# An eight-layer attention and feed-forward stack on one core: moved waits, a shared expert first on batch 0, batch 1 normalised later

## The reference, cut to what matters

```
x = x + L0_xattn(layernorm(x), ctx)   # top-32 attention gives FiLM factors, a state-space convolution by DFT, a GELU FFN
x = x + L0_ffn(layernorm(x))          # router picks 4 of 16 heads per batch item, then 512 x 512 self-attention
x = x + L1_xattn(layernorm(x), ctx)   # one head; scores normalised by mean and variance over the whole batch item
x = x + L1_ffn(layernorm(x))          # ternary signatures pick one of 64 table rows per token (argmax of a spline gate, twice)
x = x + L2_xattn(ctx, layernorm(x))   # two heads, x attends to x and to the context
x = x + L2_ffn(layernorm(x))          # 8 experts, top 2 weighted by softmax, plus 2 shared experts, hidden 256
x = x + L3_xattn(layernorm(x), ctx)   # 16 heads, 77 keys
x = x + L3_ffn(layernorm(x))          # ternary weights, hidden 512, GELU, layernorm inside
```

## Time and profile before

| what | value |
|---|---|
| median of three timed runs | 590.55 us (587.39, 590.55, 593.42) |
| the profiled execution's own time | 593.67 us |
| its span, first to last instruction | 591.9 us |
| mean granted TensorE clock | 0.896 of full speed |
| busy: TensorE matmul, VectorE, ScalarE, GpSimd | 86%, 65%, 46%, 26% |

### The profile page before, as it was taken

One profiled execution on the slowest core, in us unless ns is written; L12 is line 12 of the kernel. 1 busy time (PEld: TensorE's weight loads), 2 busy tenths in 40 slices (PEclk: granted clock), 3 DMA queues, 4 the chain that ended last, 5 costly groups with the idle time before them and its releaser, 6 DMA issues.

```text
span 591.9 us, 9329 instructions
## 1 busy us (share of the span) xinstructions
PE 510.3 (86%) x3141; PEld 351.9 (59%) x3141; DVE 383.6 (65%) x1362; ACT 272.2 (46%) x842; POOL 152.2 (26%) x179
## 2 busy tenths in 40 slices
PE   4931899999888999988879779989999999789976
PEld 2310899896434667765455457755666666358845
DVE  4899979466763668437666547753444444689766
ACT  2887675404135666432424426622222221678553
POOL 5999970301380000003004600100000000200042
PEclk9665599999989999998858959969999999789989
DMA  7002000003540000000001120000000000000001
GB/s 275 30 18 125 2 2 2 1 1 142 234 176 0 3 1 2 2 1 0 20 14 43 41 56 1 2 1 2 1 1 0 1 0 2 1 1 0 3 0 37
DMA packets 8198, 18.37 MB, mean 31 GB/s; under 512 B 1044, under 2 KB 6228, under 8 KB 7639
## 3 DMA queue, kind: packets, MB, share of 16 engines
q1 hardware_dynamic: 8150, 17.78, 8.4%
HBM read 15.99 MB, written 1.79 MB: 30 GB/s over the span
## 4 chain that ended last, share of the span: by engine, by line
PE 63%; DVE 14%; POOL 12%; ACT 5%; issue 3%; DMA 1%; SPq 0%; DVEq 0%; POOLq 0%; ACTq 0%
PE bank L1779 6%; PE bank L1780 6%; PE bank L1790 6%; PE bank L248 3%; PE bank L1026 3%; PE bank L1965 3%; PE bank L765 3%; PE bank L1070 3%; PE bank L1049 2%; PE bank L1941 2%; ACT arenaB L1981 2%; POOL rstd L206 2%; DVE stats L197 2%; PE bank L1653 2%; PE bank L679 2%
## 5 line engine op out<-in xcount | busy, mean ns | idle before, releaser
L205 POOL TENSOR_SCALAR rtmp<-mv 128x4 f32<-128x4 f32 x22 | 5.1, 230 | 326.3 <-DVE mv L191 326.3
L1831 DVE TENSOR_TENSOR arenaB<-arenaB,bank 128x512 f32<-128x512 f32 x40 | 27.5, 688 | 55.0 <-PE bank L1780 54.1
L1801 ACT ACTIVATE arenaB<-bank 128x512 f32<-128x512 f32 x40 | 23.9, 598 | 77.0 <-PE bank L1779 77.0
L1790 PEld LDWEIGHTS bank<-arenaA,arenaB 128*128 128x128 f32 x320 | 38.7, 192 | 9.1 <-issue 9.1
L248 PE MATMUL bank<-in_ctx 128*128 128x512 f32 (+1 forms) x114 | 43.4, 528 | 0.0
L1779 PE MATMUL bank<-xnT,arenaA 128*128 128x512 f32 x80 | 42.8, 618 | 0.0
L1780 PE MATMUL bank<-xnT,arenaA 128*128 128x512 f32 x80 | 42.0, 607 | 0.0
L1790 PE MATMUL bank<-arenaA,arenaB 128*128 128x128 f32 x320 | 38.8, 275 | 0.0
L248 PEld LDWEIGHTS bank<-in_ctx 128*128 128x128 f32 x114 | 20.2, 210 | 17.7 <-issue 17.6
L1981 ACT ACTIVATE arenaB<-bank,arenaB 128x77 f32<-128x77 f32 x88 | 27.2, 345 | 7.6 <-DVE arenaB L2004 7.6
L1780 PEld LDWEIGHTS bank<-xnT,arenaA 128*128 128x128 f32 x80 | 15.8, 197 | 20.2 <-issue 20.2
(11 more groups left out here) (472 smaller groups left out, 1260.8 us busy)
## 6 DMA issues: line engine op xcount, KB each, us to landing
arenaA<-in_moe_dram SPq DMA_DIRECT2D x1, 3840.0 KB, 11.7
in_dft<-in_dft_dram SPq DMA_DIRECT2D x1, 2048.0 KB, 7.4
in_dft<-in_head_dram SPq DMA_DIRECT2D x1, 2048.0 KB, 7.5
arenaA<-in_l_dram SPq DMA_DIRECT2D x1, 2048.0 KB, 16.2
vw_scratch<-in_dft SPq DMA_DIRECT2D x32, 38.5 KB
arenaB<-vw_scratch SPq DMA_DIRECT2D x2, 576.0 KB, 4.9
in_rows<-in_rows_dram SPq DMA_DIRECT2D x1, 842.5 KB, 7.3
in_ctx<-in_ctx_dram SPq DMA_DIRECT2D x1, 653.0 KB, 4.9
```

Of the source, the lines that this page charges most:

```text
L1790: ins = nc.tensor.matmul(bank[4 + m % 3][:, q4 * P:(q4 + 1) * P], hid2[:, m % 2, c, q4 * P:(q4 + 1) * P], w[:, 2 * HE + c * P:2 * HE + (c ...
L1801: nc.scalar.activation(sil2[:, n % 3, :], bank[n % 2][:], ACT.Silu).then_inc(silu_ready, 1)
L1831: Vv.tensor_tensor(hid2[:, m % 2, c, :], sil2[:, n % 3, :], bank[2 + n % 2][:], ALU.mult).then_inc(hid_ready, 1)
```

## The change

1. **Route.** The context keys are scaled, transposed and copied inside the route (`vec_c2_scale` after L930, `pe_c2_keys` after L915, `act_c2_keys` after the Exp). The spins are 2 and 5 calls instead of 3 and 8. The values of batch 1 are computed at step n = 1 of `attend0`, whose first wait is then for queries and keys alone. GpSimd waits for `heads_ready` before `pool_bias(3)` and the ternary weights.
2. **Moments.** A new `vec_tile_moments` does one tile's statistics. In `attend0`, `attend2` and `attend3` batch 1's moments are taken tile by tile inside the loop.
3. **L1_xattn.** Batch 0's copy and output product come before the last tiles; additions and moments go by batch item; the spin after it is 3 calls, not 4.
4. **L1_ffn.** The addition for `comp` and the second Exp each stand ahead of what was before them (`first_best`, `fold3` chunk 0); one spin of 2 calls is gone; both transposes precede all table products.
5. **L2_xattn into L2_ffn.** Batch 0 is normalised and turned inside `attend2` (steps 8 and 9). The experts start with shared expert 8 on batch 0; batch 1 is turned at step 2, the router products stand at step 4, and the choice of the best two is spread over steps 4 to 7 of VectorE's loop; its Exp becomes a power on GpSimd.
6. **L3.** `vec_normalise(9, [1])` moves from ahead of `attend3` into its step 1, after tile 0's product; `vec_normalise(10, [1])` into step 1 of `l3f`. Batch 0's turn for `l3f` goes into `attend3`'s last step.
7. **Stores.** Three groups of four: batch 0, batch 1's first two tiles, its last two.

```diff
+        def vec_tile_moments(st, src, t):
+            st.link(nc.vector.bn_stats(stats[:, t, :], src[:, t, :]))
+            ins = nc.vector.bn_aggr(mv[:, t, :], stats[:, t, :])
+            if t % TB == TB - 1:
+                ins.then_inc(ln_moments, 1)
...
-            pe_spin(6, 3)
+            pe_spin(6, 2)
             pe.wait_ge(route_vec, 1)
             nc.tensor.transpose(bank[4][0:NB, 0:HF], dist[:], ident[0:HF, 0:HF]).then_inc(route_pe, 1)
-            pe_spin(6, 8, S)
+            pe_c2_keys(pe)
+            pe_spin(6, 5, S)
...
             pe.wait_ge(qk_ready, 8)
-            pe.wait_ge(v_ready, 4)
-            pe_c2_keys(pe)
             for n in range(NU + 3):
...
+                if n == 1:
+                    pe_v0(pe, 1)
...
+                if n > 2 * TB + 4 and n % 2:
+                    t = (n - 5) // 2
+                    dve.wait_ge(x_added, t + 1)
+                    vec_tile_moments(st, X, t)
...
@@ def pe_l1x(pe), def act_l1x(act), def vec_l1x(dve, st)
+                if t == NT - 2:
+                    pe_l1x_out(pe, 0)
+            pe_l1x_out(pe, 1)
...
+                if t == NT - 3 or t == NT - 1:
+                    b = t // (NT - 1)
+                    act.wait_ge(e1_turned, b + 1)
+                    nc.scalar.copy(pT1[:, b * S:(b + 1) * S], bank[4 + b][0:NC, :]).then_inc(pT1_ready, 1)
...
+            for b, r in enumerate(halves()):
+                dve.wait_ge(e1_ready, TB * (b + 1))
+                st.link(Vv.reciprocal(ri1[:, r], rs1[:, r]))
+                dve.wait_ge(y1_mm, b + 1)
...
+                vec_moments(st, X, [b])
...
@@ def pe_l1f(pe), def act_l1f(act), def vec_l1f(dve, st)
             pe_fold3(pe, *FOLD3[0])
-            pe_spin(1, 2, S)
             pe_fold3(pe, *FOLD3[1])
...
                 ins.then_inc(l1f_pe, 1)
+            for b in range(NB):
+                pe.wait_ge(l1f_act, 6 + b)
                 for m in range(b * TB // 2, (b + 1) * TB // 2):
-                    pe.wait_ge(l1f_act, 6 + 3 * b)
...
-            act_fold3(act, *FOLD3[0])
             act.wait_ge(l1f_vec, 3)
             nc.scalar.activation(sg, cand, ACT.Exp, scale=-1.0).then_inc(l1f_act, 1)
+            act_fold3(act, *FOLD3[0])
             act_fold3(act, *FOLD3[1])
...
             vec_gates(st)
-            first_best(st, ga, b81, ocl)
             dve.wait_ge(l1f_pe, 5)
             Vv.tensor_tensor(comp[:], bank[6][:, 0:2 * NT].rearrange("p (t c) -> p t c", c=2), bm(V["cb2"], NT), ALU.add).then_inc(l1f_vec, 1)
+            first_best(st, ga, b81, ocl)
...
@@ def pe_attend2(pe), def vec_attend2(dve, st)
+                if n == NT + 1:
+                    pe_turn(pe, ln_done, NT * 8, xn, [0])
...
+                if n > TB + 3:
+                    dve.wait_ge(x2_added, n - 3)
+                    vec_tile_moments(st, X, n - 4)
+                if n == NT:
+                    vec_normalise(dve, 8, X, xn, [0])
...
+        EXPERTS = (NE,) + tuple(range(NE)) + (NE + 1,)
+        TURN8 = (0, 7)
...
+                if n == 0:
+                    pe.wait_ge(ln_T, NB * 6 + 1)
+                    pe.wait_ge(*loaded["moe"])
+                if n == 2:
+                    pe_turn(pe, ln_done, NT * 8, xn, [1], TURN8)
+                    pe.wait_ge(ln_T, NB * 6 + 2)
+                if n == 4:
+                    for t in range(NT):
+                        ins = nc.tensor.matmul(bank[7][:, t * NE:(t + 1) * NE], xnT[:, t * P:(t + 1) * P], V["router"], start=True, stop=True)
+                    ins.then_inc(lg_mm, 1)
...
+        def pool_moe(pool):
+            pool.wait_ge(lg_diff, 1)
+            nc.gpsimd.tensor_tensor(e2x[:], V["euler"].broadcast_to([P, NT]), e2x[:], ALU.pow).then_inc(lg_exp, 1)
...
@@ def vec_moe(dve, st)
+                if n == 4:
+                    vec_best_two(dve, st)
+                if n == 5:
+                    vec_best_places(st)
+                if n == 6:
+                    vec_best_weights(dve, st)
+                if n == 7:
+                    vec_combine(st)
...
@@ def vec_attend3(dve, st)
                     Vv.tensor_tensor(p3[:, t % 3], p3[:, t % 3], bc(sm3[:, t % 3], P, H3, NC), ALU.mult).then_inc(s3_norm, 1)
+                if n == 1:
+                    vec_normalise(dve, 9, X, xn, [1])
...
@@ def pe_attend3(pe)
+                if n == NT + 2:
+                    pe.wait_ge(s3_exp, 3 * NT)
+                    pe_turn(pe, ln_done, NT * 10, xn, [0])
...
+        STORES = ((0, 0, TB), (1, 0, TB // 2), (1, TB // 2, TB))
...
+            for b, q0, q1 in STORES:
+                sp.wait_ge(x4_added, b * TB + q1)
+                for g, r in enumerate(quarters()):
+                    sp.dma_start(tokens(out, g)[:, b, q0:q1], X[r, b * TB + q0:b * TB + q1]).then_inc(stored, 16)
...
@@ the lists of TensorE and GpSimd
-            pe_spin(2, 4, S)
+            pe_spin(2, 3, S)
...
+            pool.wait_ge(heads_ready, NB)
             pool_bias(pool, 3, V["bo0"], row_added)
```

More of the change, by code:

```diff
@@ L997, in act_qk0, with vec_v0 @@
                         n += 1
-        def vec_v0(dve):
-            vec_c2_scale(dve)
-            for m in range(4):
-                b = m // 2
+        def vec_v0(dve, b):
+            for m in range(2 * b, 2 * b + 2):
                 dve.wait_ge(v_mm, m + 1)
@@ L1202, in pe_l1x, with pe_l1x_out @@
                     ins.then_inc(e1_turned, 1)
-            for b in range(NB):
-                pe.wait_ge(pT1_ready, b + 1)
-                for q4 in range(TB):
-                    t = b * TB + q4
-                    ins = nc.tensor.matmul(bank[6 + b][:, q4 * P:(q4 + 1) * P], pT1[:, t * P:(t + 1) * P], vw1[:, b, :],
-                                           start=True, stop=True)
-                ins.then_inc(y1_mm, 1)
+                if t == NT - 2:
+                    pe_l1x_out(pe, 0)
+            pe_l1x_out(pe, 1)
+        def pe_l1x_out(pe, b):
+            pe.wait_ge(pT1_ready, b + 1)
+            for q4 in range(TB):
+                t = b * TB + q4
+                ins = nc.tensor.matmul(bank[6 + b][:, q4 * P:(q4 + 1) * P], pT1[:, t * P:(t + 1) * P], vw1[:, b, :],
+                                       start=True, stop=True)
+            ins.then_inc(y1_mm, 1)
         def act_l1x(act):
@@ L1764, in program @@
         up_mm, silu_ready, hid_ready, down_mm, moe_added = sem("up_mm"), sem("silu_ready"), sem("hid_ready"), sem("down_mm"), sem("moe_added")
+        EXPERTS = (NE,) + tuple(range(NE)) + (NE + 1,)
+        TURN8 = (0, 7)
         def pe_moe(pe):
[L1767 to L1773 removed]
+            for n in range(4 * NX + 2):
+                if n == 0:
[8 more added lines that the diff above has]
+                    ins.then_inc(lg_mm, 1)
                 if n < 4 * NX:
[L1775 removed]
+                    e, b, c = EXPERTS[n // 4], n // 2 % 2, n % 2
                     w = V["moe"][:, e * WE:(e + 1) * WE]
@@ L1794, in act_moe @@
         def act_moe(act):
-            act.wait_ge(lg_diff, 1)
-            nc.scalar.activation(e2x[:], e2x[:], ACT.Exp).then_inc(lg_exp, 1)
             for n in range(4 * NX):
+                if n % 2 == 0 and n < 4:
+                    act_turned(act, 6, which=[n // 2], banks=TURN8)
                 act.wait_ge(up_mm, 2 * n + 1)
@@ L2280, in _ @@
             act_qk0(act)
-            act_c2_keys(act)
             act_attend0(act)
```

132 lines of the change are left out of this document (64 added, 68 removed).

## The result

The changed kernel takes 575.52 us (median of 4 executions, 575.28 to 576.00), the kernel before 591.33 us beside it (587.39 to 593.42): the ratio is 0.9736, with a 95% interval of 0.9687 to 0.9784 (here and below the ratio is estimated from the single executions, so it is not exactly the quotient of the two medians). Run a second time as a control it took 575.44 us (574.14 to 577.27), ratio 0.9721 (0.9652 to 0.9790). The forecast was 574.8, which is 15.75 us of saving; the medians differ by 15.8. That agreement is closer than the working deserves, as the stages show.

The account below looks back on a forecast made before the run. TensorE, busy 86% of the span, was taken to bound the kernel, the rest being handover between sublayers. Terms 4.3 + 0.85 + 0.5 + 4.0 + 5.5 - 1.5 + 1.9 + 0.2 = 15.75 off 590.55 gave 574.8 us, range 568 to 583.

Parts of the forecast that it names:

- (a): Route: with GpSimd behind `heads_ready`, L927 takes some 0.2 us instead of 1.61, 1.4 less.
- (b): Route: keys and a shorter spin of 6.2 us before the queries, which start 2.6 us earlier (2.2 to 3.3).
- the first rival: The clock takes half back through new gaps or dropped spins, ternary weights slowing VectorE beside attend0: 581 us, chance 0.21.
- (c): Before attend0's scores: waits and batch 1's values go, 2.2 us; the values at step 1 cost 0.5; net 1.7.
- Part 2: attend0: tile-by-tile moments take statistics off the path after the last addition, 0.85 us less; nothing freed in attend2 and attend3.
- Part 3: L1_xattn: batch 1's normalise ends at 271.7 instead of 272.4 and the spin shortens; 0.5 us less.
- Part 4: L1_ffn: VectorE's chain starts earlier and ends 6.0 us earlier, 2 given back in L2_xattn; net 4.0 (3.4 to 6).
- Part 5: L2_xattn into the experts: a new wait of 1.4 us, step 4 6.35 us earlier; 5.5 taken in case the clock drops.
- Part 6: L3: batch 1's turn waits for the moved normalise, 1.5 us lost (nearer 2.7 by the clock page); then 1.9 won in L3_ffn.
- Part 7: Stores at the end: 32 KB transfers instead of 128, the landing of 2.2 us shortens little; 0.2 us less (0 to 0.5).
- The clock rival: New gaps or dropped spins in parts 1, 4, 5 and 6 let the clock take half back: 581 us, chance 0.21.
- the slower rival: attend0 falls to half clock behind shorter spins and a gap; all of it slow gives 604 us, chance 0.03.

Follow-up runs that it names:

- a_pool_early: The changed kernel without GpSimd's wait for the heads; 577.33 us, ratio 0.9798.
- b_pool_wait: The kernel before with GpSimd's wait for the heads alone; 586.17 us against 594.15, ratio 0.9885.
- b_l1_ffn: The kernel before with the L1_ffn edits alone; 584.06 us against 592.72, ratio 0.9892.
- a_long_spin: The changed kernel with 11 calls of the spin instead of 5 in front of L2_xattn's turn; 572.86 us, ratio 0.9722.
- a_turn_later: The changed kernel with L2_xattn's turn of batch 0 moved behind the last tile's values; 573.29 us, ratio 0.9726.
- the three b_ variants: The kernel before with GpSimd's wait alone (586.17 us), the L1_ffn edits alone (584.06 us), or the edits from L2_xattn into the experts alone (583.86 us).
- a_norm_front: The changed kernel with batch 1's normalise of L3_xattn put back in front of the loop; 572.12 us, ratio 0.9693.
- a_combo: The changed kernel with a_norm_front's, a_long_spin's and a_turn_later's edits together; 571.90 us, ratio 0.9677.

## Why the prediction was right

The terms against the pair of profiles (starts in the two timelines, the route's 0.31 of a later start taken out; part 4 is taken to L2_xattn's main scores, 345.71 before and 336.74 after):

| part | forecast | pair | what the variants say |
|---|---|---|---|
| 1 route | 4.3 | 5.2 | 2.3 to 5.2, by the clock under the router products and the spins |
| 2 tile moments | 0.85 | 0.8 | |
| 3 L1_xattn | 0.5 | -0.1 | about 0.4 on the mean of all profiles |
| 4 L1_ffn | 4.0 | 3.3 | 1.4 slow stretch in this profile |
| 5 to the experts | 5.5 | 6.5 | 6.9 and 8.2 alone |
| 6 L3_xattn | -1.5 | -0.1 | -1.3, by undoing it |
| 6 L3_ffn | 1.9 | 2.5 | 1.1 to 2.5 |
| 7 stores | 0.2 | 0.7 | 0.6 to 0.7 |
| sum | 15.75 | 18.6 (without the later start 18.9) | |

**Part 1.** (a) L927 at 0.2 was right, and a_pool_early and b_pool_wait show its cause. (b) The forecast took a mixed clock under the spin, 6.2 us; it ran at full clock, 4.50, and the heads became the bound, the end of the range that it named (the queries are 3.56 closer to the turn of batch 0, against 3.3 at that end). The Trainium skill's page SBUF — State Buffer, section Who interferes with whom, says that the engine which comes second is blocked until the first is done; the trace agrees for L927 (1.61 us, to the end of GpSimd's tensor_tensor). Beside the ternary weights attend0 took no longer (58.00 us with them and 57.99 without), so the blocking that part 1 put into the first rival did not come. (c) 1.67 for 1.7.

**Part 2** was right: batch 1's normalise starts 2.54 us behind batch 0's turn instead of 3.31, 0.8 closer.

**Part 3** can't be read from the pair. From attend0's first transposes to L1_ffn's first product the four profiles without parts 2 and 3 took 81.0 to 81.9 us and the ten with them 79.4 to 80.8; the means differ by 1.2, and part 2 has 0.8 of it. It was not tested alone.

**Part 4.** The mechanism was right at each step that was named: gates 0.3 us behind L1401 (now L1425), full clock over the table products, a new gap in front of the turn. Two sizes were off in this profile: the chain came 4.6 earlier, since the short products and the spin ahead of the fold took 1.6 us more at half clock (2.63 and 6.34 for 1.94 and 5.40), which b_l1_ffn did not have; and the gap gave back 1.3, not 2, which a_long_spin shows.

**Part 5.** The new wait was there (1.3 us on the last values: they are 7.96 ahead of before, where tile 6's were 9.26), and a_turn_later takes 0.76 of it back. I subtracted about 0.9 from 6.35 for a gap that would put the clock down at the turn of batch 1; it was 0.68 and did not. Up to step 4 the pair gives 6.8, where the working had 6.35 before the subtraction; later steps take 0.3 of it back. The largest piece in both is the clock, which the working named for the router alone: it put the steps before step 4 at full clock as well, and the end of half clock there is some 4.5 us. That the shorter waits are what keeps the clock up fits all fourteen profiles; it was not tested apart from the new order.

**Part 6.** The mechanism was right: the turn waits, TensorE idles 3.73 us, undoing it wins 1.3. The half clock behind the gap came as well (3.68 us for six scores), so the trace agrees with the sentence that the forecast took from the Trainium skill, page TensorE: Matmul & The Clock Gate, section What's actually happening. The 2.7 that the forecast drew from it did not come: undoing the edit wins 1.3. In the pair it costs 0.1, since the profiled execution of before had its own slow stretches in L3a (25.24; in three more profiles of the same code 22.31 to 25.23). The failing step was to take that single execution for the kernel: each of its dips was counted as if it came every time. The router's dip did come every time; those of L3_xattn did not.

**Part 7** was mis-sized: the smaller landing, 1.6 for 2.2, was put at little, and it is the whole term.

**The sum.** The pair gives 2.8 us more than forecast, and the medians do not. The profiled execution of before took 593.67 us, 2.3 above its median. A part of the errors therefore cancels, by luck, because I took the saving off the median while working from a slower execution. The clock rival did not come as a whole: full clock was kept at three of the edges and lost at two, in front of L2_xattn (1.3 us) and of L3_xattn's tile 2 (3.68 us for six scores instead of 2.24). Attend0 stayed at full clock (58.00 for 58.05 us), so the slower rival had no ground. Two slips in the prediction did no harm. The adverse end of part 4 (3.4) leaves out the case that its own text prices, a chain only 3.7 earlier with up to 2.6 given back. And the slow stretch from 298 to 315 was not half idle: TensorE was busy for 14.72 of its 17 us.

## What to carry to other kernels

When a normalise or a transpose is moved behind other work, look for what stands behind its turn in TensorE's program: here two moves that were good in their own stage each made a wait (0.78 and 3.73 us), and undoing the one and putting the turn of the other one group of products later gave 2 us by the stages. Look, too, for products behind an old gap: of the 6.8 us won up to step 4 of the experts, some 4.5 are half clock that is gone. Fill a new gap in front of dense products with work of no use, but only where those products are the bound: it won 1.3 us in front of L2_xattn and 0.45 us in L3_xattn. Before a term of 1 us is read from two profiles, compare stages that did not change; here they differ by up to 3.

## What the runs showed of the hardware that was not expected

- The savings of single parts may not add up to that of the whole. The medians of the three b_ variants are 8.0, 8.7 and 8.9 us below those measured beside them, 25.5 together, where the whole change, which holds these and more, gives 15.8 to 17.3. By the ratios the three are 6.8, 6.4 and 6.7 us, each with an interval of 2.5 us or more to either side, and their sum of 19.9 is not told apart from the whole. In the profiles, stages with unchanged code are faster by up to 2.9 (L3a) and 1.4 us (L3b), where products of the kernel before ran at half clock. That a small shift moves these stretches fits the profiles; what decides it was not tested.
- Four scores took 1.56, 2.33, 2.39 and 2.86 us at the same place of L3_xattn in different executions (b_l1_ffn, a_norm_front, a_combo, before). The clock changes in the middle of a group, and at another place each time: in a_norm_front the half clock begins within this group (granted clock 0.80 in its first 1.1 us, then 0.50, and 1.00 from 509.5 on), in the kernel before it ends behind it (0.53 in the group, 0.69 in the transposes that follow).
- VectorE was held by GpSimd's tensor_tensor in more places than the route: beside L927 and L1531 above, also in the kernel before, where L410 handles 128x8 elements in 1.20 us and ends at 67.44, when L633 on GpSimd ends at 67.42:

```profile
66.24 1.20 DVE L410 TENSOR_SCALAR nb<-arenaB 128x8 f32<-128x8 f32 x1
```
```profile
66.15 1.27 POOL L633 TENSOR_TENSOR arenaB<-arenaB 128x512 f32<-128x512 f32 x1
```

  Beside GpSimd's tensor_scalar of 2.0 us VectorE was slowed, but not held to its end. Its three SCALAR_TENSOR_TENSOR of the route took 0.99 together in the kernel before, and 0.74 in b_pool_wait and in the changed kernel, where GpSimd does nothing beside them:

```profile
169.97 0.99 DVE L939 SCALAR_TENSOR_TENSOR gsel<-in_rows,gidf,gsel 2x16 f32<-2x16 f32 x3
```
```profile
169.74 2.01 POOL L2076 TENSOR_SCALAR in_l3f<-in_l3f,wgam 128x512 f32<-128x512 f32 x1
```
